# A three-stage decoder layer: the slot stage with four groups in turn, the new-gate products ahead of the z products, and the new gate's tanh in the same beat

## The reference

```
repeat 3 times:
    sn     = rmsnorm(slots);  scores = (sn Wq^T)(Pn Wk^T)^T * SCALE
    attn   = softmax over the slots, then divided by its sum over the context
    upd    = attn (Pn Wv^T)
    r, z   = sigmoid(upd Wr + h Ur), sigmoid(upd Wz + h Uz)
    n      = tanh(upd Wn + r * (h Un));   slots = (1 - z) * n + z * h
x = layernorm(x + slots); route = sigmoid(x Wr + br); expert = argmax(route)
```

## Time and profile before

| | |
|---|---|
| median of 3 runs | 1671.12 us (1670.48 to 1673.46) |
| the profiled execution's own time | 1671.58 us |
| its span | 1669.4 us |
| slot stage, first to last instruction | 917.97 to 1478.29 us |
| PE / DVE / ACT / POOL busy in the span | 89% / 76% / 66% / 75% |

### The profile page before, as it was taken

One profiled execution on the slowest core, in us unless ns is written; L12 is line 12 of the kernel. 1 busy time (PEld: TensorE's weight loads), 2 busy tenths in 40 slices (PEclk: granted clock), 3 DMA queues, 4 the chain that ended last, 5 costly groups with the idle time before them and its releaser, 6 DMA issues. The chain is left out here.

```text
span 1669.4 us, 22143 instructions
## 1 busy us (share of the span) xinstructions
PE 1489.2 (89%) x6336; PEld 908.0 (54%) x6336; DVE 1262.5 (76%) x2184; ACT 1105.3 (66%) x2134; POOL 1246.7 (75%) x884
## 2 busy tenths in 40 slices
PE   4889899989999999989987999999999999929994
PEld 1334334433443343433432777777777777729993
DVE  2999999999999999999996466666666675644552
ACT  4778887788778887888775665556556565414553
POOL 2899999999999999999996435666566655534665
PEclk8999999999999999999999899999999999959997
DMA  5455555554555455555551840412403310036771
GB/s 175 136 192 183 164 175 176 180 173 158 198 165 187 156 180 193 182 163 176 169 174 44 269 167 17 154 44 111 154 25 130 103 48 14 7 87 189 214 208 39
DMA packets 126058, 236.93 MB, mean 142 GB/s; under 512 B 13490, under 2 KB 76917, under 8 KB 125952
## 3 DMA queue, kind: packets, MB, share of 16 engines
q1 hardware_dynamic: 121408, 227.21, 41.8%
q0 software_dynamic: 4544, 8.47, 1.5%
HBM read 180.89 MB, written 55.66 MB: 142 GB/s over the span
## 5 line engine op out<-in xcount | busy, mean ns | idle before, releaser
L388 POOL TENSOR_TENSOR hc<-state,c_rows 128x1024 f32<-128x1024 f32 x256 | 599.1, 2362 | 50.0 <-DVE state L585 40.3
L585 DVE TENSOR_TENSOR_SCAN state<-ps_da,inp 128x512 f32<-128x512 f32 x512 | 593.5, 1207 | 29.6 <-ACT ps_da L481 29.6
L704 PE MATMUL ps_y<-hc,ident 128*128 128x512 f32 x1024 | 495.1, 623 | 55.5 <-POOL hc L388 55.4
L481 ACT ACTIVATE ps_da<-dt,a_neg 128x512 f32<-128x512 f32 x512 | 345.1, 688 | 81.7 <-DVE state L585 79.2
L704 PEld LDWEIGHTS ps_y<-hc,ident 128*128 128x128 f32 x1024 | 195.6, 198 | 298.8 <-issue 214.7
L574 DVE TENSOR_TENSOR inp<-dtx,ps_b 128x1024 f32<-128x1024 f32 x192 | 230.9, 1203 | 39.3 <-POOL dtx L359 23.0
L998 POOL TENSOR_TENSOR rs<-ms,m_half 128x4 f32<-128x4 f32 x48 | 49.7, 1035 | 186.4 <-DVE ms L1201 186.4
L371 POOL TENSOR_TENSOR inp<-dtx,b_rows 128x1024 f32<-128x1024 f32 x64 | 150.9, 2358 | 0.1
L627 PE MATMUL ps_misc<-x1T,w_conv 128*128 128x512 f32 (+3 forms) x256 | 118.6, 608 | 20.9 <-ACT x1T L414 20.9
L487 ACT COPY ps_b<-b_rows 128x512 f32<-128x512 f32 x192 | 111.1, 579 | 36.6 <-DVE inp L574 35.1
L1662 POOL DMA_INDIRECT out_x<-orow,target x78 | 77.0, 987 | 43.4 <-ACT orow L1681 23.7
(11 more groups left out here) (214 smaller groups left out, 2759.9 us busy)
## 6 DMA issues: line engine op xcount, KB each, us to landing
b_rows<-bc_rows SPq DMA_DIRECT2D x128, 512.0 KB, 4.7
c_rows<-bc_rows SPq DMA_DIRECT2D x128, 512.0 KB, 4.0
sorted_x<-pad_rows SPq DMA_DIRECT2D x8, 4160.0 KB, 16.3
w<-in_L_ffn_W SPq DMA_DIRECT2D x78, 256.0 KB
vw<-vw_rows SPq DMA_DIRECT2D x16, 462.0 KB
vw_rows<-vw_out SPq DMA_DIRECT2D x16, 384.0 KB
xrow<-sorted_x SPq DMA_DIRECT2D x39, 130.0 KB, 2.3
x_tok<-in_x SPq DMA_DIRECT2D x16, 256.0 KB, 4.0
```

The source lines that it names most:

```text
L388: pool.tensor_tensor(hc[:, n % RING], state[:, n % RING], over_c(c_rows[:, slot, n % 2]), ALU.mult).then_inc(hc_ready, 1)
L481: act.activation(ps_da[u % DA_RING][:], dt[:, par, c], ACT.Exp, scale=a_neg[:, c, n:n + 1]).then_inc(da_ready, 1)
L585: dve.tensor_tensor_scan(state[:, n % RING, c], ps_da[u % DA_RING][:], inp[:, n % RING, c], 0.0, ALU.mult, ALU.add).then_inc(state_ready, 1)
L704: ins = pe.matmul(ps_y[:, c], ident[:], hc[:, n % RING, c], start=False, stop=n == NS - 1)
```

## The change

Units now come as (four groups) x (three iterations), the groups taking turns: beat n brings unit n into attention. Its softmax is finished in beat n+1 (`den`, `den_spread`, `weights`), its gates in beat n+2, its new state in beat n+3, and `square(n+1)` in that beat starts the group's next iteration, four beats after the last. The `keep_running` products go. In the gates' beat, PE makes xn before z and ACT takes the new gate's tanh before z's. State, `kq`, `vw` and `ctx_r` get rings of 8 groups; the first iteration reads `x1T` without a copy. The post work of a group is laid over beats R to R+6, with R three beats after its last unit plus a spread, which makes one group per three beats; the last four groups have R = 47, 48, 49 and 50. `ps_s` now has a bank of its own, and so have the spread roots (`ps_rs`) and the denominators (`ps_d`, shared with `ssq`); what is left for `ps_u` is one bank, in which `make_u` writes two halves in turn and `count` its columns. The context sums of groups 2 to 15 are laid out by `root_at`.

```diff
+    FOUR = 4
+    units = [(q * FOUR + k, j) for q in range(NG // FOUR) for j in range(ITERS) for k in range(FOUR)]
+    place_of = {unit: n for n, unit in enumerate(units)}
...
+    for g in range(NG):
+        spread = 2 * (g % FOUR) if g < NG - FOUR else 0
+        ready[place_of[g, ITERS - 1] + 3 + spread] = g
+    LAST = N + 9
...
-    ps_u = [psum(f"ps_u{k}", [P, T]) for k in range(2)]
+    ps_u = psum("ps_u", [P, T])
+    COUNT_AT = 2 * (P + NE)
...
+    def root_at(g):
+        return g - 1 if g < FOUR else (g // FOUR - 1) * ROUND + ITERS * (g % FOUR) + 1
+    def ctx_parts(n):
+        for g in range(2, NG):
+            if n == max(0, root_at(g) - 2):
+                yield g, range(0, 2)
+            if n == max(0, root_at(g) - 1):
+                yield g, range(2, GB)
...
@@ SP: after kq, vw and ctx of groups 0 to 3
-        for k in range(2):
-            load_ctx(1, k)
-            load_kq(1, k)
-            load_vw(1, k)
         sp.wait_ge(const2, 18)
         sp.dma_start(xs_spare, pad.broadcast_to([P, 2, PER * XROW])).then_inc(spare_padded, 16)
         clear_page(0)
+        for g in range(FOUR, RING):
+            load_ctx(g)
+            load_kq(g)
+            load_vw(g)
...
@@ POOL, each beat
+            root(n); halve(n - 2); residual, g = post(n, 0); scatter, post(n, 6)
+            normed, post(n, 4); logits, post(n, 2); labels, post(n, 5); root_ctx
...
@@ ACT
+        square(0)
+        sum_ctx(0, range(GB))
+        sum_ctx(1, range(GB))
...
+        for n in range(LAST):
+            if live(n):
+                copy_scores(n)
+            if live(n - 2):
+                gate_hn(n - 2)
+                gate_r(n - 2)
+            g = post(n, 1)
+            if g is not None:
+                read_u(g, 0)
+            if live(n + 1):
+                square(n + 1)
+            if live(n):
+                exps(n)
+            if live(n - 2):
+                gate_new(n - 2)
+                gate_z(n - 2)
+            if g is not None:
+                read_u(g, 1)
...
+                route_tanh(g)
+            for g, batches in ctx_parts(n):
+                sum_ctx(g, batches)
...
@@ DVE, each beat
+            mean_sq(n); statistics, post(n, 2); kept, mixed, new_h (n - 3)
+            maxima(n); denominators(n - 1); reset, new_in (n - 2); weights(n - 1)
+            highest, chosen_expert, last_norm, post(n, 4)
+            ranks, destinations, post(n, 5); normaliser(n)
...
@@ PE
+        def count(g):
+            k, n = g % 2, NE * GB
+            need(pe, u_read, made_u[0])
...
+        for n in range(LAST):
+            if live(n - 2):
+                gate_hn(n - 2)
+                gate_h(n - 2, 0, ps_r, r_read)
+                gate_x(n - 2, 0, ps_r, r_full, True)
+            if live(n):
+                root_spread(n)
+            if live(n - 1):
+                den(n - 1)
+            if live(n - 2):
+                need(pe, pre_done, n - 2)
+                gate_x(n - 2, 2, ps_xn, xn_full, False)
...
+                make_u(g, 0)
+            if live(n - 1):
+                den_spread(n - 1)
+            if live(n - 2):
+                gate_h(n - 2, 1, ps_z, z_read)
+                gate_x(n - 2, 1, ps_z, z_full, True)
+            if g is not None:
+                make_u(g, 1)
+            g = post(n, 4)
+            if g is not None:
+                count(g)
+            if live(n + 1):
+                ssq(n + 1)
+                scores(n + 1)
```

More of the change, by code:

```diff
@@ L786, in slot_stage @@
     at = [sb(f"at{k}", [M, T]) for k in range(2)]
+    half = [sb(f"half{k}", [P, T]) for k in range(2)]
     hnb = sb("hnb", [P, T])
@@ L826, in slot_stage @@
     ps_xn = psum("ps_xn", [P, T])
-    ps_u = [psum(f"ps_u{k}", [P, T]) for k in range(2)]
[L830 to L840, removed]
+    ps_u = psum("ps_u", [P, T])
+    COUNT_AT = 2 * (P + NE)
+    MOMENTS = ["stats", "mv"]
+    CHOICE = ["top", "less", "cand", "which", "hot", "upto"]
+    RANKS = ["based", "base", "chosen", "dest_f"]
+    LOGITS = ["veps", "rstd", "scaled", "logits"]
+    LABELS = ["gate", "id", "next_id"]
+    MAXIMA = ["s", "mx", "nmx"]
+    INVERSE = ["rse", "rser"]
+    STATE = ["keep", "mix", "h"]
+    w_in_place = sem("slot_w_loaded")
     const2 = sem("const2")
@@ L874, in u_value @@
[L874 to L902, removed]
+    def ev(names, name, n):
+        return after(len(names), names.index(name), n)
+    def live(n):
+        return 0 <= n < N
+    def post(n, late):
+        return ready.get(n - late)
+    def h_in(n):
+        g, j = units[n]
+        return x1T[:, g * T:(g + 1) * T] if j == 0 else h[g % RING][:]
@@ new lines, in _ @@
+        for n in range(LAST):
+            if live(n):
+                root(n)
+            if n == 0:
+                root_ctx(0)
+                root_ctx(1)
+            if live(n - 2):
+                halve(n - 2)
+            g = post(n, 0)
+            if g is not None and g < NG - 1:
+                residual(g)
+            g = post(n, 6)
+            if g is not None and g < NG - 2:
+                scatter(g)
+            g = post(n, 4)
+            if g is not None and g < NG - 2:
+                normed(g)
+            g = post(n, 2)
+            if g is not None:
+                logits(g)
+            g = post(n, 5)
+            if g is not None:
+                labels(g) if g < NG - 2 else last_labels(g)
+            for g in ctx_roots(n):
+                root_ctx(g)
@@ L1507, in _ @@
-        over_pairs(pe, body)
-        it = NQ * ITERS - 1
-        pe.wait_ge(post_v[1], ev(POSTV, "base", NQ - 2))
-        gate_x(1, it, 1, "r")
-        gate_x(1, it, 1, "z")
-        gate_x(1, it, 1, "xn")
-        for lane in range(2):
-            make_u(NQ, lane)
-        count(0, NQ - 1, 1, it)
-        pe.wait_ge(post_v[0], ev(POSTV, "base", NQ - 1))
-        count(1, NQ - 1, 1, it)
+        pe.wait_ge(w_in_place, 16 * 4)
+        pe.matmul(ps_u[:, 0:NE], ones[:], w_r[:], start=True, stop=True).then_inc(prep_pe, 1)
```

870 lines of the change are left out of this document (406 added, 464 removed).

## The result

The changed kernel takes 1711.7 us (median of 4 runs, 1702.8 to 1713.5), against 1672.3 for the kernel before beside it: ratio 1.0226, 95% interval 1.0188 to 1.0263, slower by 2.3%. The forecast was 1704, in a range of 1676 to 1722. The profiled execution took 1712.5, with a span of 1710.5 (before 1669.4).

The account below looks back on a forecast made before the run. PE's queue was taken to set the stage's pace. Beats gain 47.8; start loses 20.6, end 39.5, clock 20: 1703.9 from 1671.6, forecast 1704 us, 2.0% slower, range 1676 to 1722.

Parts of the forecast that it names:

- The beats: Slot stage, third L1206 to a 49th: ordinary beats 9.4, third beats with `count` 12.5; gain 47.8 us.
- The clock: PE in the 11 beats with `count`: most fall to low clock after the wait, 1.8 each, 20 us lost.
- The start: ACT's beat 0: group 4's context load waits for the cleared page; loss 20.6 us, about 7 if it slips through.
- The end: Behind the last beat: four groups' post work instead of two, carried by POOL in order; loss 39.5 us.
- The sum: Whole kernel: 1671.6 - 47.8 + 20.6 + 39.5 + 20 = 1703.9 us against the profiled execution.
- A (clock holds): PE in the beats: no falls of the clock, so 1684 us, slower by 0.8%; chance 0.17.
- B (`count` is not held): Third beats: ACT's reads do not hold `count`, 21 more goes, 1663 us (1650 with free start); chance 0.11.
- C (the context slips past): Start: group 4's context load passes the page, 7 lost instead of 20.6, 1690 us; chance 0.12.
- D (every fall at full price): Beats with `count`: falls cost 33 or more instead of 20, 1717 to 1725 us; chance 0.15.

Follow-up runs that it names:

- three combined ones: Changed kernel with context sums, `count` and last norms later: 1644.7 us; plus norms of groups 12 and 13 sooner: 1636.5; plus group 4's load first: 1638.4.
- gap-filled kernel: Changed kernel with two unread 512-column products put ahead of `count`, where TensorE waits for ScalarE: 1689.7 us, ratio 1.0113.

## Why the prediction was right

**The beats.** Predicted 9.4 for an ordinary one and 12.5 for a third one; measured 9.39 to 9.6 and, at full clock, 12.33 to 12.35. The gain of 47.8 was 47.8, once the falls are taken out; that it agrees to the tenth is luck, since the ordinary beats took 1.6 more in all and the third ones 1.9 less. The reason held too: `count` waited for the second `tok`, if for 1.5 to 1.7 and not 1.9, and with `count` where nothing holds it a third beat is 9.8 to 10.3. The headline order does its work: putting z first again lengthens the ordinary beat by 1.6. The part that I did not price apart, the tanh's place, is worth nothing here.

**The clock.** 20 predicted (1.8 for each of 11), 20.0 measured, but made up in another way: 3 beats passed without a fall, 4 lost 1.7 and 4 lost 3.3. The sum fitted by the average of a mix, and that is luck too: I had expected falls shorter than the 3.0 of the earlier trace rows, and four of the eight cost 3.3. Filling the gap gave it back whole. That these 20 are the clock's is shown; which beats fall and which pass is not. In the profiles of the kernels that keep the wait and the order, 6 to 8 of the 11 beats have a fall, for 13 to 23 us in all. The times fit that in part: the runs of these kernels lie 8 to 12 us apart, those of the three combined ones 1.3 to 2.0. But those of the gap-filled kernel lie 7.0 apart, with no fall in the beats of its profile, so something else moves them as well, and what it is stays open.

**The start.** 20.6 predicted, 22.6 measured in that execution and 19.0 in the profile of the kernel with `count` later, whose start is the same (the slot stage began 0.7 later than before in the one and 0.5 earlier in the other). The choice between 20.6 and 7 was settled as I had chosen: the load let the page pass. By the rule of the Trainium skill on queues (DMA: Bandwidth & Descriptors, Queues, rings and completion order), each DMA engine takes one issuer's descriptors in their order; the trace agrees, with 15.7 us from issue to use behind the page and 2.8 ahead of it.

**The end.** The term that was mis-sized: 39.5 predicted, 44.9 measured (I had named 45 as the upper end, for a low clock). The step is GpSimd's queue behind the last beats: up to the scatter of group 12 I added its work with one pause, 1.9 for the state, and came to 38.6 behind the mark; it took 47.1 (1502.4 less 1455.3). The trace shows GpSimd idle 2.57 (the state), 3.85 and 3.85 (`mv` L1297). The two latter come from the ring of two `tok` buffers: rows of group g, read of g + 2, `statistics`, logits of g + 2. I had the queue, not the loop. In the other direction, `normed` is 3.15 here, not 3.7 to 3.9 (why is not shown), and a scatter's landing, which I took as 2.9 from a row of another stage, takes 1.5 and 1.4 (1502.42 to 1503.94, 1512.21 to 1513.63): 2.9 less for the two. So the missing loop was worth more than the 5.4 that the sum is off by.

**The sum.** Of the 8.6 us between 1703.9 and the profiled execution's 1712.5, the end makes 5.4, the start 2.0, the rest of the span about 1.5.

**The rivals.** A (clock holds) is refuted: 0.95 over the beats, and 8 falls. By the rule of the Trainium skill (TensorE: Matmul & The Clock Gate, HAM oscillation) idle time between bursts brings the falls; the gap-filled kernel agrees, with none left. What the rival took to be too short a wait, 1.5 to 1.7 us, was enough in 8 beats of 11. B (`count` is not held) did not happen but was built: 1662.4, against the 1663 that I gave it. That is closer than its terms were: the beats came out 3.6 better than my 47.8 and 21 together, and the start 1.6 better, the end 4.7 worse. C (the context slips past) is refuted by the wait of 15.2. D (every fall at full price) had four of its eleven.

## What to carry over

Before changing the order of a tuned queue, list each wait that it makes on the engine that sets the pace, and price it at more than its length: here 1.5 to 1.7 us of waiting cost that, and by the falls of the clock 1.8 more on average. The change as it stood lost 2.3%, and its gain of 48 us was real all along: small moves of work that has slack (sums, `count`, and the norms in two places) brought it out at 2.1% faster. And when more chains run in turn, price their common start and their common end apart from the beats; they were 67 of the losses here.

## What the hardware showed that I had not expected

Useless work made a kernel faster: 2 x 11 products of 512 columns, put into a wait, took 19.9 us off the beats. A fall behind `count` costs one of two amounts, 1.7 or 3.3, in every kernel that keeps the wait and the order. And a fall is possible almost without idle time: one, with 0.22 us of wait behind `count`, in one of four profiled kernels with `count` later. What decides there stays open.
